# State space heads of a two-layer decoder: the squares of a group summed on VectorE ahead of one product with ones, and the decay block off the diagonal made by ScalarE alone

## The chip, the cores and the metric

The kernel runs on one core of a Trainium2 chip. The metric is the device time of one execution in microseconds (us). A core has TensorE (PE in the profile; PEld are its weight loads), VectorE (DVE), ScalarE (ACT), GpSimd (POOL) and SyncE (SP), each with a queue of its own, which run their instructions in order and wait for one another by semaphores.

## The reference, cut to what matters

A decoder of two layers on 8 sequences of 256 tokens with 256 channels: a state space mixer, cross attention and a gated layer, then self attention, cross attention and a layer of 64 experts, each with a layer norm behind it. Only the first, the state space mixer, is touched by the change. It has 32 heads of 128 channels in 8 groups of norms:

```python
proj = x @ in_proj_w.T
gate, hbc, dt = jnp.split(proj, [I, I + CD], axis=-1)
hbc = silu(conv(hbc, width 4) + conv_b)
hs, B, C = jnp.split(hbc, [I, I + G * N], axis=-1)
dt = softplus(dt + dt_bias); A_bt = -exp(A_log) * dt
# per head, with cum the running sum of A_bt over a sequence:
#   y[l] = sum over s <= l of (C[l] . B[s]) * exp(cum[l] - cum[s]) * dt[s] * X[s]  +  D * X[l]
...
gs = I // G                       # 512 channels, 4 heads
h32 = y * silu(gate)
g = h32.reshape(b, s, I // gs, gs)
var = jnp.mean(g * g, axis=-1, keepdims=True)
h32 = (g * rsqrt(var + EPS)).reshape(b, s, I)
return norm_w * h32 @ out_proj_w.T
```

The line on y is a summary: the reference works it out in chunks of 32 tokens, and the kernel over all 256.

## The kernel before

`mamba_stage` runs `mamba_dt` (dt and its running sums, as rows `cum_rows` in memory and as columns `dtc`), then two passes, each of `mamba_bc` (the masked products C.B into `cb`) and `mamba_heads` (4 groups of 4 heads). The stage takes the first 1280 us; what follows is not touched.

`mamba_heads` goes in steps: a step is one group and one pair of sequences (n counts steps, 16 in a pass), and in it four turns, one for each head j. `head_turns` writes the loop, `slot` gives each engine in each turn its parts, each for a head so many turns ahead: TensorE `project` (3 ahead), `scan` (1), `turn` (2), `out` (0); ScalarE `decays` (2), `square` (0), `activate` (3), `weigh` (2), `tanh` (3); VectorE `finish` (0), `silu` (2), `conv` and `open_` (3); GpSimd `match` (2), `argue` (3). This order, written by hand, is the order of each queue.

For one head: `project` makes px (the head's channels) and pz (its gate), each two products of 512 columns. ScalarE makes pre from px and tz from pz, VectorE runs three taps of the convolution on pre (`conv_taps`), and makes gate from tz and xs from tx, ScalarE's tanh of pre. `turn` transposes xs into pxt, and `weigh` scales it by dt/2 to xt. GpSimd's `argue` writes the arguments cum[l] - cum[s], with the smaller of that and 0 taken, into `decay`, ScalarE takes the exponential in place, and GpSimd's `match` multiplies with `cb` into mix. The block of a sequence is 256 source tokens by 256 targets, of which 384 columns are kept: columns 0 to 255 (`0:S`) are source tokens 0 to 127 with all targets, columns 256 to 383 (`S:TRI`) source tokens 128 to 255 with the second 128 targets. So columns 128 to 255 (`P:S`) are the block off the diagonal. `scan` multiplies xt with mix to py, `finish` makes y and h = y x gate, `square` makes sq = h^2, and `out` adds to po (h times the output weights) and to pss, the sum of squares over channels, by a product of sq with a column of ones.

At the start of a step VectorE reads pss of the last step (`variance`), GpSimd makes the root (`root`), and VectorE scales po with it and adds to x_rows (`add`). GpSimd's `group` at a group's start makes h_d and h_wo from the new weights, and y of head 0 waits for it. SyncE loads the running sums (`cum`) into two buffers cumb, and the weights of each group.

Of the kernel before, what the change touches and what calls it, by code (L numbers as in the profile page):

```python
# [108 lines left out]
def mamba_stage(nc, a, r):  # L109

    with ExitStack() as ctx:
        def sb(name, shape, dt=F32):
            return ctx.enter_context(nc.sbuf_tensor(name, shape, dt))

        def sem(name):
            return ctx.enter_context(nc.semaphore(name))  # L120

        cum_rows = nc.dram_tensor("cum_rows", (H, T), F32, kind="Internal").ap()
        cb = sb("cb", [P, NP * GH, 2, TRI])
        dtc = sb("dtc", [P, NT, 2 * H])
        mamba_dt(nc, a, r, cum_rows, dtc)
        for half in range(2):
            mamba_bc(nc, a, r, half, cb)
            mamba_heads(nc, a, r, half, cum_rows, dtc, cb)


def mamba_dt(nc, a, r, cum_rows, dtc):

    with ExitStack() as ctx, ExitStack() as ctx2:
# [62 lines left out]
        def _(dve):  # L196
# [242 lines left out]
def mamba_heads(nc, a, r, half, cum_rows, dtc, cb):  # L439
# [9 lines left out]
    with ExitStack() as ctx, ExitStack() as ctx2:  # L449
# [20 lines left out]
        cumb = [sb(f"cumb{i}", [P, HG, 2, S]) for i in range(2)]  # L470
        sel = [sb(f"sel{i}", [P, TW, 2, HG]) for i in range(2)]
        decay = [sb(f"decay{i}", [P, 2, TRI]) for i in range(HG)]
# [58 lines left out]
        def _(sp):  # L531
# [9 lines left out]
            def cum(s):  # L541

                sp.wait_ge(argued, LEAD + (s.n - 1) * HG)
                sp.dma_start(cumb[s.vb][:].rearrange("p j u l -> p j (u l)"),
                             cum_rows[bass.ds((s.g * 2 + half) * HG, HG), bass.ds(s.p * 2 * S, 2 * S)].partition_broadcast(P)).then_inc(cums[s.vb], 16)
# [10 lines left out]
        def _(pool):  # L556
# [12 lines left out]
            def argue(s, j, h):  # L569

                pool.wait_ge(cums[s.vb], (s.g * (NP // 2) + s.two + 1) * 16)
                pool.wait_ge(picked, LEAD + s.n + 1)
                for u in range(2):
                    pool.tensor_scalar(decay[j][:, u, 0:S], cumb[s.vb][:, j, u, :], sel[s.vb][:, u * TPB, 1, j:j + 1], 0.0,  # L574
                                       ALU.subtract, ALU.min)
                    ins = pool.tensor_scalar(decay[j][:, u, S:TRI], cumb[s.vb][:, j, u, P:S], sel[s.vb][:, u * TPB + 1, 1, j:j + 1], 0.0,  # L576
                                             ALU.subtract, ALU.min)
                ins.then_inc(argued, 1)
# [27 lines left out]
        def _(pe):  # L606
# [36 lines left out]
            def out(s, j, h):  # L643
                pe.wait_ge(finished, LEAD + h + 1)
                pe.wait_ge(squared, LEAD + h + 1)
                if j == 0:
# [3 lines left out]
                for t in range(TW):  # L650

                    pe.matmul(po[t // TPB][:, t % TPB, :], hh[j % 2][:, t * P:(t + 1) * P], w_out[s.pg][:, j, :],  # L652
                              start=(j == 0 and t % TPB == 0), stop=(j == HG - 1), skip_group_check=True)
                    mm = pe.matmul(pss[:, t:t + 1], sq[j % 2][:, t * P:(t + 1) * P], r.ones[:, 0:1],  # L654
                                   start=(j == 0 and t == 0), stop=(j == HG - 1), skip_group_check=True)
                mm.then_inc(outed, 1)
# [12 lines left out]
        def _(act):  # L669
# [49 lines left out]
        def _(dve):  # L719
            for one in po:  # L720
                dve.memset(one[:], 0.0)
            dve.memset(pss[:, 0:TW], 0.0)
            for one in (picked, convolved, opened, silued, finished):
                dve.drain().then_inc(one, LEAD)
# [26 lines left out]
            def finish(s, j, h):  # L751
# [23 lines left out]
            def body(prev, cur, nxt):  # L775
                for j in range(HG):
# [2399 lines left out]
```

## Time and profile before

| what | value |
|---|---|
| time, median of 3 runs | 3485.99 us (3485.69 to 3489.45) |
| profiled execution, its own time | 3490.39 us |
| its span, first to last instruction | 3488.6 us |
| granted TensorE clock over the span | 0.833 |
| TensorE busy | 2766.1 us, 79% |
| VectorE, ScalarE, GpSimd busy | 1854.6 us (53%), 1553.7 us (45%), 1204.1 us (35%) |
| the squares' products, 1024 instructions, first and last start | 180.0 and 1280.8 us |

The busy shares are means over stages that differ; the two passes over the heads lie from 151 to 665 us and from 769 to 1284 us. A product of 32-bit numbers is two instructions to TensorE, each with a weight load, so the profile counts 1024 where the code has 512.

### The profile page before, as it was taken

Reading aid. Unit: us, or ns where it says so; the run is one execution under the profiler, and the core shown is the slowest. Engines: PE = TensorE matmul, PEld = TensorE weight load, DVE = VectorE, ACT = ScalarE, POOL = GpSimd, SP = SyncE. Lnnn points to the kernel's source line nnn. Section 1 sums busy time; section 2 is a strip of 40 time slices with the busy share of each in tenths; the row PEclk is TensorE's granted clock in tenths of the full one; section 3 lists DMA queues with packets and bytes.
Section 4 is the critical chain, followed back from the end, with each engine's and each line's share of the span. In section 5 each row is a group of like instructions: output and inputs, shape, how many; then the busy total and the mean of one; then the engine's idle time right before and its main releaser. Section 6 shows DMA issues by size and latency. Waiting matters only on the chain. (4 is left out here: it accounts for less than half of the span.)

```text
span 3488.6 us, 49109 instructions
## 1 busy us (share of the span) xinstructions
PE 2766.1 (79%) x13661; PEld 1696.1 (49%) x13663; DVE 1854.6 (53%) x4142; ACT 1553.7 (45%) x3112; POOL 1204.1 (35%) x1132
## 2 busy tenths in 40 slices
PE   5799999879999975887887937887477525988884
PEld 2477777646777753444444513333344212455552
DVE  4676666666666656767773156774322510222334
ACT  3555555455555543767771115665155200123331
POOL 1477777437777740000000021000100063144443
PEclk8999999989999985555557957998679755899997
DMA  1122111012122106500000000000000051377875
GB/s 61 46 55 51 34 51 37 7 49 55 27 53 55 37 12 208 170 1 0 1 1 29 0 17 1 1 1 1 21 1 0 1 179 69 69 163 169 180 172 124
DMA packets 127079, 192.70 MB, mean 55 GB/s; under 512 B 17552, under 2 KB 88208, under 8 KB 125584
## 3 DMA queue, kind: packets, MB, share of 16 engines
q1 hardware_dynamic: 83696, 134.71, 13.7%
q0 software_dynamic: 23616, 33.24, 5.4%
q10 hardware_dynamic: 19584, 22.57, 2.4%
q8 instruction: 83, 1.36, 0.2%
q14 instruction: 100, 0.82, 0.1%
HBM read 123.23 MB, written 67.25 MB: 55 GB/s over the span
## 5 line engine op out<-in xcount | busy, mean ns | idle before, releaser
L228 DVE SCALAR_TENSOR_TENSOR h_pre<-h_px,h_par,h_pre 128x510 f32<-128x510 f32 (+2 forms) x384 | 286.5, 746 | 270.6 <-ACT h_pre L689 250.7
L843 POOL TENSOR_TENSOR norm_rstd<-norm_mv,mhalf 128x4 f32<-128x4 f32 x24 | 28.2, 1177 | 1023.3 <-DVE norm_mv L826 1023.3
L652 PE MATMUL h_po<-h_wo,h_h 128*128 128x256 f32 x1024 | 329.3, 412 | 0.0
L2906 POOL DMA_INDIRECT moe_sums<-ex_y,ex_sidx x132 | 204.8, 1552 | 321.1 <-DVE ex_y L3074 302.9
L574 POOL TENSOR_SCALAR h_decay<-h_cumb,h_sel 128x256 f32<-128x256 f32 x256 | 292.0, 1141 | 25.4 <-DMA h_cumb<-cum_rows 25.4
L585 POOL TENSOR_TENSOR h_mix<-h_decay,cb 128x768 f32<-128x768 f32 x128 | 232.9, 1820 | 166.3 <-ACT h_decay L675 166.3
L616 PE MATMUL h_px<-x_cols,h_w 128*128 128x512 f32 x512 | 254.4, 620 | 25.6 <-DMA h_d<-d_skip 25.6
L1256 ACT ACTIVATE xq_ex<-xq_ps,xq_nmax,xq_qs 128x512 f32<-128x512 f32 x256 | 199.4, 779 | 113.6 <-DVE xq_nmax L1324 113.0
L621 PE MATMUL h_pz<-x_cols,h_w 128*128 128x512 f32 x512 | 242.4, 596 | 5.7 <-DVE h_gate L742 5.6
L1322 DVE TENSOR_REDUCE xq_top<-xq_ps 128x1 f32<-128x512 f32 x256 | 176.3, 689 | 83.5 <-PE xq_ps L1169 81.7
L701 ACT ACTIVATE h_xt<-h_pxt,h_sel 128x128 f32<-128x128 f32 x512 | 146.4, 369 | 152.2 <-PE h_pxt L640 152.2
L2951 PE MATMUL ex_pg<-ex_w,ex_xT 128*128 x528 | 193.5, 489 | 23.0 <-DVE ex_h L3070 8.2
L654 PEld LDWEIGHTS h_pss<-ones,h_sq 128*128 128x128 f32 x1024 | 195.1, 191 | 26.5
L1176 PE MATMUL xq_pa<-identb,xq_pr 128*128 128x128 bf16 x1024 | 149.8, 299 | 61.2 <-DVE xq_pr L1329 60.4
L576 POOL TENSOR_SCALAR h_decay<-h_cumb,h_sel 128x128 f32<-128x128 f32 x256 | 182.5, 713 | 0.0
L689 ACT ACTIVATE h_pre<-h_px,h_par 128x512 f32<-128x512 f32 x128 | 99.6, 778 | 172.6 <-PE h_px L616 165.3
L3064 DVE COPY ex_wt<-ex_xg 128x1 f32 x132 | 20.3, 154 | 274.1 <-DMA moe_sums<-ex_y,ex_sidx 271.1
L621 PEld LDWEIGHTS h_pz<-x_cols,h_w 128*128 128x128 f32 x512 | 97.6, 192 | 132.0 <-issue 121.3
L631 PE MATMUL h_py<-h_mix,h_xt 128*128 128x256 f32 x512 | 155.0, 385 | 7.2 <-DVE h_h L760 7.1
L2053 DVE TENSOR_REDUCE at_nmax<-at_pd 128x4 f32<-128x1024 f32 (+1 forms) x96 | 117.4, 1223 | 79.2 <-PE at_pd L1783 77.0
L652 PEld LDWEIGHTS h_po<-h_wo,h_h 128*128 128x128 f32 x1024 | 155.9, 192 | 0.1
L2967 PE MATMUL ex_po<-ex_wd,ex_hT 88*128 x528 | 142.7, 393 | 16.3 <-issue 13.7
(390 smaller groups left out, 6004.6 us busy)
## 6 DMA issues: line engine op xcount, KB each, us to landing
h_cumb<-cum_rows SPq DMA_DIRECT2D x32, 1024.0 KB, 8.6
moe_tiles<-blank SPq DMA_DIRECT2D x4, 6642.0 KB, 44.1
ex_w<-moe_w SPq DMA_DIRECT2D x64, 352.0 KB
ex_xg<-moe_tiles ACTq DMA_DIRECT2D x136, 162.0 KB
ex_wd<-moe_wd SPq DMA_DIRECT2D x64, 176.0 KB
h_w<-w_xg SPq DMA_DIRECT2D x8, 1024.0 KB, 10.4
moe_sums<-blank SPq DMA_DIRECT2D x2, 2176.0 KB, 26.7
h_wo<-w_out SPq DMA_DIRECT2D x8, 512.0 KB, 10.3
```

The source lines that it names most:

```text
L228: ins = dve.scalar_tensor_tensor(out=out[:, :, back:S], in0=src[:, :, 0:S - back], scalar=par[:, at + CK - 1 - back:at + CK - back], in1=o ...
L574: pool.tensor_scalar(decay[j][:, u, 0:S], cumb[s.vb][:, j, u, :], sel[s.vb][:, u * TPB, 1, j:j + 1], 0.0, ALU.subtract, ALU.min)
L576: ins = pool.tensor_scalar(decay[j][:, u, S:TRI], cumb[s.vb][:, j, u, P:S], sel[s.vb][:, u * TPB + 1, 1, j:j + 1], 0.0, ALU.subtract, ALU.min)
L585: pool.tensor_tensor(mix[j % 2][:], decay[j][:], cbj, ALU.mult).then_inc(matched, 1)
L616: mm = pe.matmul(px[j % 2][:].rearrange("p u l -> p (u l)"), w_in[s.pg][:, k, j, 0, :], r.xT[:, k, bass.ds(s.p * 2 * S, 2 * S)], start=(k ...
L621: mm = pe.matmul(pz[:], w_in[s.pg][:, k, j, 1, :], r.xT[:, k, bass.ds(s.p * 2 * S, 2 * S)], start=(k == 0), stop=(k == KE - 1))
L652: pe.matmul(po[t // TPB][:, t % TPB, :], hh[j % 2][:, t * P:(t + 1) * P], w_out[s.pg][:, j, :], start=(j == 0 and t % TPB == 0), stop=(j = ...
L654: mm = pe.matmul(pss[:, t:t + 1], sq[j % 2][:, t * P:(t + 1) * P], r.ones[:, 0:1], start=(j == 0 and t == 0), stop=(j == HG - 1), skip_gro ...
L1256: act.activation(ex[m % 4][:], ps[m % 2][:], ACT.Exp, bias=nmax[s.par][:, m:m + 1], scale=qs[s.par][:, m:m + 1], accum_out=tot[s.par][:, m ...
L1322: dve.tensor_reduce(top[:, m:m + 1], ps[m % 2][:], AX.X, ALU.max, negate=True)
L2906: pool.indirect_dma_start(out=r.sums[i % 2][:, :], out_offset=bass.IndirectOffsetOnAxis(ap=sidx[i][:, 0:1], axis=0), in_=y[i % 2][:], in_o ...
L2951: mm = pe.matmul(pgu[n][:, 0:2 * FE], xT[n][:, k, :], w[:, bass.ds(lane, 1), k, :].rearrange("p a f -> p (a f)"), start=(k == 0), stop=(k ...
```

## The change

Two edits in `mamba_heads`, and one that prepares for them in `mamba_dt`. First, `out` no longer multiplies each head's squares with ones. The square of a group's first head goes to a new tile `sqsum`, VectorE adds those of the other three heads to it (a new part `gather`, behind `silu` and ahead of `conv` in each turn but the first), and `out` of the last head multiplies the sum with ones, behind its four po. Second, `argue` leaves out the block off the diagonal, and `decays` makes it from `cumb` with the negated cum[s] as a bias, which `dtc` and `sel` hold as a third column; the exponential of the rest is one instruction over the two diagonal blocks. The load of `cumb` waits for the decays, since ScalarE reads `cumb` as well.

```diff
@@ mamba_dt
+                dve.tensor_scalar(dtc[:, 8 * i:8 * i + 8, 2 * H:3 * H], pt[i][:, :, H:2 * H], -1.0, None, ALU.mult)
@@ cum
-                sp.wait_ge(argued, LEAD + (s.n - 1) * HG)
+                sp.wait_ge(decayed, LEAD + (s.n - 1) * HG)
@@ argue
-                    pool.tensor_scalar(decay[j][:, u, 0:S], cumb[s.vb][:, j, u, :], sel[s.vb][:, u * TPB, 1, j:j + 1], 0.0,
-                                       ALU.subtract, ALU.min)
-                    ins = pool.tensor_scalar(decay[j][:, u, S:TRI], cumb[s.vb][:, j, u, P:S], sel[s.vb][:, u * TPB + 1, 1, j:j + 1], 0.0,
-                                             ALU.subtract, ALU.min)
+                    for n in range(TPB):
+                        ins = pool.tensor_scalar(decay[j][:, u, n * S:n * S + P], cumb[s.vb][:, j, u, n * P:(n + 1) * P],
+                                                 sel[s.vb][:, u * TPB + n, 1, j:j + 1], 0.0, ALU.subtract, ALU.min)
@@ out
-                pe.wait_ge(squared, LEAD + h + 1)
...
-                    mm = pe.matmul(pss[:, t:t + 1], sq[j % 2][:, t * P:(t + 1) * P], r.ones[:, 0:1],
-                                   start=(j == 0 and t == 0), stop=(j == HG - 1), skip_group_check=True)
+                if j == HG - 1:
+
+                    pe.wait_ge(summed, LEAD + (s.n + 1) * (HG - 1))
+                    for t in range(TW):
+                        mm = pe.matmul(pss[:, t:t + 1], sqsum[s.vb][:, t * P:(t + 1) * P], r.ones[:, 0:1],
+                                       start=(t == 0), stop=(t == TW - 1), skip_group_check=True)
@@ decays
-                act.activation(decay[j][:], decay[j][:], ACT.Exp).then_inc(decayed, 1)
+                own = decay[j][:].rearrange("p u (n l) -> p u n l", l=P)[:, :, 0:3:2, :]
+                act.activation(own, own, ACT.Exp)
+                for u in range(2):
+                    ins = act.activation(decay[j][:, u, P:S], cumb[s.vb][:, j, u, P:S], ACT.Exp, bias=sel[s.vb][:, u * TPB, 2, j:j + 1])
+                ins.then_inc(decayed, 1)
@@ square
-                act.wait_ge(outed, LEAD + h - 1)
-                act.activation(sq[j % 2][:], hh[j % 2][:], ACT.Square).then_inc(squared, 1)
+                if j == 0:
+                    act.wait_ge(outed, LEAD + (s.n - 1) * HG)
+                else:
+                    act.wait_ge(summed, LEAD + s.n * (HG - 1) + j - 2)
+                act.activation(sqsum[s.vb][:] if j == 0 else sq[j % 2][:], hh[j % 2][:], ACT.Square).then_inc(squared, 1)
@@ VectorE
+            def gather(s, j, h):
+                if j:
+                    dve.wait_ge(squared, LEAD + h + 1)
+                    dve.drain()
+                    dve.tensor_tensor(sqsum[s.vb][:], sqsum[s.vb][:], sq[j % 2][:], ALU.add).then_inc(summed, 1)
...
-                    slot(((3, conv), (3, open_)), cur, nxt, j)
+                    slot(((0, gather), (3, conv), (3, open_)), cur, nxt, j)
```

On TensorE, a turn of the first step before, from its transposes to the next turn's first product (L640 the transposes, L652 po, L654 pss, L616 px):

```order
L640 MATMUL h_pxt<-ident,h_xs 128x128 x4
L652 MATMUL h_po<-h_wo,h_h 128x256
L654 MATMUL h_pss<-ones,h_sq 128x1
L652 MATMUL h_po<-h_wo,h_h 128x256
L654 MATMUL h_pss<-ones,h_sq 128x1
...
L616 MATMUL h_px<-x_cols,h_w 128x512 x2
```

The same place now, in the third and the fourth turn of a step (L642 the transposes, L653 po, L659 pss, L618 and L623 px and pz, L633 and L634 py):

```order
L642 MATMUL h_pxt<-ident,h_xs 128x128 x4
L653 MATMUL h_po<-h_wo,h_h 128x256 x4
L618 MATMUL h_px<-x_cols,h_w 128x512 x2
L623 MATMUL h_pz<-x_cols,h_w 128x512 x2
L633 MATMUL h_py<-h_mix,h_xt 128x256
L634 MATMUL h_py<-h_mix,h_xt 128x128
...
L642 MATMUL h_pxt<-ident,h_xs 128x128 x4
L653 MATMUL h_po<-h_wo,h_h 128x256 x4
L659 MATMUL h_pss<-ones,h_sqsum 128x1 x4
```

Three turns of a step have only po behind the transposes, and the fourth has all four pss in a row behind its po.

On VectorE, the second turn of the first step before, from y on (L755 y, L760 h, L748 xs, L228 the taps, L742 gate):

```order
L755 SCALAR_TENSOR_TENSOR h_y<-h_xs,h_d,h_py 128x512
L760 TENSOR_TENSOR h_h<-h_y,h_gate 128x512
L748 SCALAR_TENSOR_TENSOR h_xs<-h_tx,h_pre 128x512
L228 SCALAR_TENSOR_TENSOR h_pre<-h_px,h_par,h_pre 128x2x255
L228 SCALAR_TENSOR_TENSOR h_pre<-h_px,h_par,h_pre 128x2x254
L228 SCALAR_TENSOR_TENSOR h_pre<-h_px,h_par,h_pre 128x2x253
L742 SCALAR_TENSOR_TENSOR h_gate<-h_tz,h_pz 128x512
```

The same turn now (L767 y, L772 h, L760 xs, L778 the new sum, L229 the taps, L754 gate):

```order
L767 SCALAR_TENSOR_TENSOR h_y<-h_xs,h_d,h_py 128x512
L772 TENSOR_TENSOR h_h<-h_y,h_gate 128x512
L760 SCALAR_TENSOR_TENSOR h_xs<-h_tx,h_pre 128x512
L778 TENSOR_TENSOR h_sqsum<-h_sqsum,h_sq 128x512
L229 SCALAR_TENSOR_TENSOR h_pre<-h_px,h_par,h_pre 128x2x255
L229 SCALAR_TENSOR_TENSOR h_pre<-h_px,h_par,h_pre 128x2x254
L229 SCALAR_TENSOR_TENSOR h_pre<-h_px,h_par,h_pre 128x2x253
L754 SCALAR_TENSOR_TENSOR h_gate<-h_tz,h_pz 128x512
```

The sum stands between xs and the taps, so the taps are queued behind its wait for the square.

## Rows read from the trace of the kernel before

**Rows 1.** Busy time by stretch: us, PE, PEld, DVE, ACT, POOL, clock, DMA.

```profile
1024.00:1149.00 125.00, 125.00 (x578) 89.47 (x577) 85.39 (x149) 69.44 (x145) 94.70 (x87) 1.00 0.19 47
...
299.35:330.55 31.20, 31.20 (x147) 22.32 (x146) 22.64 (x39) 17.45 (x38) 23.12 (x21) 1.00 0.20 34
```

**Rows 2.** Timeline: start us, us, engine, line; TensorE over one turn.

```profile
307.15 1.96 PE L616 MATMUL h_px<-x_cols,h_w 128*128 128x512 f32 x4
...
308.95 1.88 PE L621 MATMUL h_pz<-x_cols,h_w 128*128 128x512 f32 x4
...
310.67 0.59 PE L631 MATMUL h_py<-h_mix,h_xt 128*128 128x256 f32 x2
...
311.98 0.60 PE L640 MATMUL h_pxt<-ident,h_xs 128*128 128x128 f32 x4
...
312.41 0.60 PE L652 MATMUL h_po<-h_wo,h_h 128*128 128x256 f32 x2
...
312.85 0.28 PE L654 MATMUL h_pss<-ones,h_sq 128*128 128x1 f32 x2
...
312.99 0.68 PE L652 MATMUL h_po<-h_wo,h_h 128*128 128x256 f32 x2
...
314.95 1.96 PE L616 MATMUL h_px<-x_cols,h_w 128*128 128x512 f32 x4
```

**Rows 3.** The page's costliest groups: weight loads, additions of squares' products.

```profile
L654 PEld LDWEIGHTS h_pss<-ones,h_sq 128*128 128x128 f32 x1024 | 195.1, 191 | 26.5
```

**Rows 4.** Waits of TensorE in the first pass over heads.

```profile
PE h_py L631 <- DVE h_h L760: 3.6, 1, 3.6
PE h_pz L621 <- DVE h_gate L742: 2.8, 2, 1.8
```

**Rows 5.** Timeline, VectorE over one turn.

```profile
312.27 0.68 DVE L742 SCALAR_TENSOR_TENSOR h_gate<-h_tz,h_pz 128x512 f32<-128x512 f32 x1
...
312.87 0.74 DVE L755 SCALAR_TENSOR_TENSOR h_y<-h_xs,h_d,h_py 128x512 f32<-128x512 f32 x1
...
313.68 0.78 DVE L760 TENSOR_TENSOR h_h<-h_y,h_gate 128x512 f32<-128x512 f32 x1
...
314.39 0.68 DVE L748 SCALAR_TENSOR_TENSOR h_xs<-h_tx,h_pre 128x512 f32<-128x512 f32 x1
...
317.77 2.39 DVE L228 SCALAR_TENSOR_TENSOR h_pre<-h_px,h_par,h_pre 128x510 f32<-128x510 f32 x3 [2.70 <-ACT h_pre L689]
```

**Rows 6.** Timeline, ScalarE over one turn.

```profile
312.67 1.15 ACT L701 ACTIVATE h_xt<-h_pxt,h_sel 128x128 f32<-128x128 f32 x4 [1.21 <-PE h_pxt L640]
...
313.69 0.64 ACT L706 ACTIVATE h_tx<-h_pre 128x512 f32<-128x512 f32 x1
...
314.30 0.84 ACT L675 ACTIVATE h_decay<-h_decay 128x768 f32<-128x768 f32 x1
...
315.05 0.61 ACT L681 ACTIVATE h_sq<-h_h 128x512 f32<-128x512 f32 x1
...
316.95 0.78 ACT L689 ACTIVATE h_pre<-h_px,h_par 128x512 f32<-128x512 f32 x1 [1.29 <-PE h_px L616]
```

**Rows 7.** GpSimd's three groups of the heads, from the page.

```profile
L574 POOL TENSOR_SCALAR h_decay<-h_cumb,h_sel 128x256 f32<-128x256 f32 x256 | 292.0, 1141 | 25.4 <-DMA h_cumb<-cum_rows 25.4
L585 POOL TENSOR_TENSOR h_mix<-h_decay,cb 128x768 f32<-128x768 f32 x128 | 232.9, 1820 | 166.3 <-ACT h_decay L675 166.3
...
L576 POOL TENSOR_SCALAR h_decay<-h_cumb,h_sel 128x128 f32<-128x128 f32 x256 | 182.5, 713 | 0.0
```

**Rows 8.** Timeline: the first head's y; a group block of GpSimd; the update behind it.

```profile
174.70 0.75 DVE L755 SCALAR_TENSOR_TENSOR h_y<-h_xs,h_d,h_py 128x512 f32<-128x512 f32 x1 [3.94 <-POOL h_wo L566]
...
297.35 1.90 POOL L566 TENSOR_TENSOR h_wo<-h_wo,h_par 128x1024 f32<-128x1024 f32 x1
...
302.39 1.66 DVE L771 SCALAR_TENSOR_TENSOR x_rows<-h_po,h_rstd,x_rows 128x256 f32<-128x256 f32 x4 [0.62 <-POOL h_rstd L590]
```

**Rows 9.** One line's instructions: min, median, max ns, 180 to 1270 us.

```profile
L760 DVE TENSOR_TENSOR h_h<-h_y,h_gate x125: 691/693/873, 183.1 to 1269.2; 128x512 f32<-128x512 f32 x125
```

More of the change, by code:

```diff
@@ L123, in mamba_stage @@
         cb = sb("cb", [P, NP * GH, 2, TRI])
-        dtc = sb("dtc", [P, NT, 2 * H])
+        dtc = sb("dtc", [P, NT, 3 * H])
         mamba_dt(nc, a, r, cum_rows, dtc)
@@ L470, in mamba_heads @@
         cumb = [sb(f"cumb{i}", [P, HG, 2, S]) for i in range(2)]
-        sel = [sb(f"sel{i}", [P, TW, 2, HG]) for i in range(2)]
+        sel = [sb(f"sel{i}", [P, TW, 3, HG]) for i in range(2)]
         decay = [sb(f"decay{i}", [P, 2, TRI]) for i in range(HG)]
@@ L483, in mamba_heads @@
         sq = [sb(f"sq{i}", [P, 2 * S]) for i in range(2)]
+        sqsum = [sb(f"sqsum{i}", [P, 2 * S]) for i in range(2)]
         var = sb("var", [P, TW])
@@ L511, in mamba_heads @@
         squared = sem("squared")
+        summed = sem("summed")
         outed = sem("outed")
@@ L650, in out @@
                 for t in range(TW):
-                    pe.matmul(po[t // TPB][:, t % TPB, :], hh[j % 2][:, t * P:(t + 1) * P], w_out[s.pg][:, j, :],
-                              start=(j == 0 and t % TPB == 0), stop=(j == HG - 1), skip_group_check=True)
-                    mm = pe.matmul(pss[:, t:t + 1], sq[j % 2][:, t * P:(t + 1) * P], r.ones[:, 0:1],
-                                   start=(j == 0 and t == 0), stop=(j == HG - 1), skip_group_check=True)
+                    mm = pe.matmul(po[t // TPB][:, t % TPB, :], hh[j % 2][:, t * P:(t + 1) * P], w_out[s.pg][:, j, :],
+                                   start=(j == 0 and t % TPB == 0), stop=(j == HG - 1), skip_group_check=True)
+                if j == HG - 1:
[3 more added lines that the diff above has]
+                                       start=(t == 0), stop=(t == TW - 1), skip_group_check=True)
                 mm.then_inc(outed, 1)
@@ L722, in _ @@
             dve.memset(pss[:, 0:TW], 0.0)
-            for one in (picked, convolved, opened, silued, finished):
+            for one in (picked, convolved, opened, silued, finished, summed):
                 dve.drain().then_inc(one, LEAD)
@@ L730, in select @@
                     ins = dve.tensor_copy(sel[s.vb][:, t, :, :],
-                                          dtc[:, bass.ds(s.p * TW + t, 1), :].rearrange("p a (c h) -> p (a c) h", c=2)[:, :, bass.ds((s.g * 2 + half) * HG, HG)])
+                                          dtc[:, bass.ds(s.p * TW + t, 1), :].rearrange("p a (c h) -> p (a c) h", c=3)[:, :, bass.ds((s.g * 2 + half) * HG, HG)])
                 ins.then_inc(picked, 1)
```

## The prediction, made before the changed kernel had run

> **What bounds the kernel now.** I read the busy time by stretch first. In a stretch from the middle of the second pass over the heads TensorE is busy for the whole 125.00 us at a granted clock of 1.00, while VectorE has 85.39 us of work, ScalarE 69.44 and GpSimd 94.70 [rows 1]. One step (two batch items, one group of four heads) is 31.20 us long and TensorE is busy for 31.20 of them [rows 1]: the reader is to see that no other engine sets the pace. The waits say the same: over 505 us of the first pass TensorE waited 3.6 us once and 2.8 us twice [rows 4].
>
> So the time of the heads is the sum of what TensorE issues, and I price that from its timeline over one turn (one head of a step). From one px to the next is 7.80 us [rows 2]: px 1.80 (307.15 to 308.95), pz 1.72 (to 310.67), py 1.31 (to 311.98), the four transposes 0.43 (to 312.41), and `out`, four pairs of po and pss, 2.54 (to 314.95). There are 128 turns in 32 steps.
>
> **What leaves TensorE.** pz streams two products of 512 columns in 1.72, so a product of 256 columns is 0.43, and the four of po should be 1.72. That leaves 2.54 - 1.72 = 0.82 for the four pss. px, the product behind the last pss, takes 1.80 where its twin pz takes 1.72; I put these 0.08 to pss too. A turn without pss is then 1.72 + 1.72 + 1.31 + 0.43 + 1.72 = 6.90 us, 0.90 less. Three turns of each step lose it: 96 x 0.90 = 86.4 us.
>
> The fourth turn keeps four pss, now back to back, which no row shows. Each is two instructions with a weight load each, 1024 loads for 512 products [rows 3]. The nearest rows are the transposes, which also load weights for each: 0.43 for four, 0.11 each [rows 2]. Eight take 0.88, and with the 0.08 for px the turn is 6.90 + 0.96 = 7.86, which is 0.06 more than now. From below, a pair takes 0.14 from its start to the next po [rows 2]; four take 0.56, the turn 0.32 less, and 10 us are gained on top. From above, a load lasts 0.191 us [rows 3]; with nothing overlapped eight take 1.53, the turn 0.65 more again, and 32 x 0.65 = 21 us of the gain are gone. I take 0.11, since a pss between po products now costs a pair 0.20 of TensorE's time, which is two of these. Step: 3 x 6.90 + 7.86 = 28.56 against 31.20. Term: 32 x 2.64 = 84.5 us.
>
> Here a page has another figure. The Trainium skill ("TensorE: Matmul & The Clock Gate", Back-to-back issue gap) gives about 81 ns for each pair of weight load and 128-column matmul in a sustained stream; the row here has 0.11. By the page the eight would take 0.65 and the whole gain would be an estimated 7 us larger; the measurement decides.
>
> **What comes to VectorE.** Each of the turns 1 to 3 gets one sum of 128x512, both operands in SBUF, with a drain ahead. Its like is h = y x gate, 693 ns in the median [rows 9], 0.71 from start to start [rows 5]. VectorE's turn today, start to start: gate 0.60, y 0.81, h 0.71, xs about 0.65, three taps 2.3; that is 5.1 of 7.80, and with the sum 5.8 to 5.9 of 6.90. Cover: VectorE now stands idle for 2.70 us ahead of the taps, waiting for ScalarE's pre [rows 5]. Behind the sum in the queue stand the taps and gate of the head three ahead, and TensorE's next pz waits for gate.
>
> Does the sum end before pre does? Count from the start of a px. The transposes begin at 4.75 in the shorter turn, and ScalarE's four xt follow 0.69 later as now (311.98 to 312.67): at 5.44. xt takes 1.02 to the next start, tx about 0.55 [rows 6], so the decays start at 7.0. Today decay, 768 columns, takes 0.75 to the next start. Its new form is one call of 512 columns (like the square, 0.61 long, about 0.52 to the next start) and two of 128 (like xt, 1.02 / 4 = 0.255): 1.03, 0.28 more. Bound from above: pre has bias and scale by partition and takes 0.78, 0.17 more than the square; with 0.17 on both calls, 0.34 more. The square then starts at 8.03 and ends at 8.64, which is 1.74 of the next turn. h was done at about 7.3, so it is not late. The sum runs from about 1.85 to 2.6. pre starts at 2.00, when px has landed, and the taps at 2.82 as now (317.77 against 314.95). The sum fits with 0.2 to spare. If it is 0.3 late, the taps end at 5.5 and gate at 6.2, and pz of the next turn wants gate at 8.62: 2.4 us of cover. py of the next turn wants h at 10.35 and has it at 7.6. I cost the sum and the calls at nothing. Without this cover each would cost its length: 96 x 0.75 = 72 us and 128 x 0.28 = 36 us.
>
> The square of turn 0 goes to the sum's own tile. TensorE no longer waits for the squares, except in turn 3: the sum is there at 2.6 of the turn, pss wants it at 6.9.
>
> **GpSimd.** A head's arguments are now four of 128 columns instead of two of 256 and two of 128: 2 x (1141 - 713) = 856 ns less; the other 713s stay and the mix, 1820, too [rows 7]. A turn goes from 5.53 to 4.67 us. Steady, this is worth nothing, since the mix is ready almost a turn before py. It counts in the ramp of each pass: the first head's y waits for GpSimd's last piece in the opening, h_wo, with VectorE idle for 3.94 us [rows 8], and TensorE's one long wait, 3.6 us, is for the h that follows [rows 4]. On that chain lie two argument blocks behind the first decay (-1.71) and two decays on ScalarE, 0.28 to 0.35 longer (+0.65): 1.0 us sooner, twice: 2 us. The new negated copy in dtc is two small VectorE instructions once, under 0.68 each (the 512-column gate [rows 5]): up to 1 us, and I take 0.7.
>
> **What gets tight.** In a group's first step the update of x_rows, whose wait is for GpSimd's root, ends at 302.39 + 1.66 = 304.05 [rows 8]; the step starts at 299.35 [rows 1], so this is at 4.70, and `out` of turn 0, which waits for it, is at 5.26 now and at 5.18 after. The group's first y waits for h_wo; GpSimd's group block comes behind turn 3's arguments, and by the sum above (decays until 1.13, mix 1.82, arguments 2.85, group block with h_wo's 1.90 [rows 8] about 2.05, a hand-over of 0.1) ends at 7.95 of a turn of 7.86, where now it ends 0.1 ahead of the turn's end (299.25 against 299.35): 0.2 later. The update is then at 4.9: 0.3 spare, in 8 steps of 32. The loads of cumb now wait for the decays instead of the arguments, 2 to 4 us later in a double-buffered ring with a step of 28 us: nothing.
>
> **Sum.** 84.5 + 2.0 - 0.7 = 85.8 us. The profiled execution took 3490.39 us for a span of 3488.60, and the median of the timed runs is 3485.99, 4.4 lower; the saving is the same against each: span 3403, profiled time 3405, median **3400 us**.
>
> **Rivals.**
> (a) The forecast: TensorE stays the bound. 3390 to 3412 by the bounds of the fourth turn (0.56 for its pss at the low end, half of the unoverlapped loads at the high one). Chance 0.80.
> (b) VectorE and GpSimd get in each other's way. For: the sum is a second instruction per turn with two SBUF operands, and GpSimd works 68% of a turn. If a sum were held back for a whole mix, 1.82, it would end at 4.4, the taps at 6.8, gate at 7.4, h at 9.0, and the round over square, sum and taps would be about 7.1 for 6.90: 96 x 0.2 = 19 us lost, 3419; with every VectorE instruction of this sort held as well, up to 3440. Against: h itself is such an instruction and in 125 cases beside a busy GpSimd was at 693 in the median and 873 at most [rows 9], so the hold is at most 0.18. The Trainium skill ("SBUF — State Buffer", SBUF: two separate sides) calls the port pair an exclusive lock between a VectorE instruction with two SBUF inputs and a GpSimd instruction that reads SBUF; these rows show no such block. Chance 0.10.
> (c) The back-to-back pss overlap nothing: 3400 + 21 = 3421. Chance 0.06.
> (d) Slower than before: ScalarE. The round taps, tx, decays, square, sum, taps is 2.39 + 0.64 + 1.03 + 0.61 + 0.75 and four hand-overs of about 0.1, 5.8 us. It decides from the point where it passes 6.90 and ends slower beyond 7.80, that is if the three decay calls take 3.0 instead of 1.03. At 1.1 us each the turn is 8.1 and the time 3486 + 128 x 0.3 = 3524. For: nothing here has a bias on a decay. Against: pre has one, at 0.78 for 512 columns [rows 6]. Chance 0.03.
> (e) No change: something else holds the turn at 7.80 even now. Against: TensorE busy for 31.20 of 31.20. Chance 0.01.
>
> **Range.** (a) with half of (b) and (c): 3390 to 3422. A change of 0.2% (7 us) is about what a measurement tells here. Faster 0.96, same 0.01, slower 0.03.
>
> **What would show it.** Turns 6.90 apart in three of four and about 7.86 in the fourth; pss 256 instructions instead of 1024, starts 0.11 apart; TensorE still busy for whole stretches at clock 1.00; the sum at about 0.7 us, ending before the taps are released by pre. Wrong would be: waits of TensorE for gate or h in each turn, VectorE waiting for the square beyond pre's end, taps that follow the sum and not pre, GpSimd's rows longer, or a fourth turn above 8.3.

## The result, and the profile after

The changed kernel takes 3441.77 us (median of 4 runs, 3434.61 to 3448.74) against 3487.72 for the kernel before beside it (3485.69 to 3490.55): ratio 0.9868, 95% interval 0.9846 to 0.989. It is faster by 46 us, little more than half of the 86 that were forecast, and lies above the range.

| | before | after |
|---|---|---|
| profiled execution, its own time | 3490.39 us | 3442.29 us |
| span | 3488.6 us | 3440.4 us |
| TensorE clock over the span | 0.833 | 0.827 |
| TensorE, VectorE, ScalarE, GpSimd busy | 2766.1, 1854.6, 1553.7, 1204.1 us | 2692.6, 2039.9, 1601.5, 1169.4 us |
| first px to last px, first and second pass | 491.9, 493.3 us | 465.7, 468.1 us |

The last line is read from the timeline of TensorE's products px, 64 a pass, and serves for all comparisons below: it holds the two passes and nothing of the stages behind them. A step should have fallen from 31.20 to 28.56 us. In the first pass 15 steps from px to px are 28.52 to 31.88, most of them 29.0 to 29.5.

VectorE's busy time grew by 185 us, where 96 sums of 0.69 are 66. Busy time by stretch, in the middle of the two passes (us, TensorE, its loads, VectorE, ScalarE, GpSimd, clock, DMA), against [rows 1]:

```profile
182.50:616.00 433.50, 426.64 (x1771) 290.18 (x1769) 400.63 (x582) 276.50 (x647) 331.06 (x314) 1.00 0.20 46
771.00:1210.00 439.00, 429.29 (x1772) 290.70 (x1773) 404.15 (x587) 277.23 (x650) 333.31 (x318) 1.00 0.19 45
```

TensorE is no longer busy all the time: 426.64 of 433.50 and 429.29 of 439.00. VectorE is at 92%. Three of the page's costliest groups, against [rows 7] (GpSimd's arguments, its mix, and the new sum):

```profile
L578 POOL TENSOR_SCALAR h_decay<-h_cumb,h_sel 128x128 f32<-128x128 f32 x512 | 398.9, 793 | 26.2 <-DMA h_cumb<-cum_rows 26.2
...
L587 POOL TENSOR_TENSOR h_mix<-h_decay,cb 128x768 f32<-128x768 f32 x128 | 264.3, 2064 | 159.8 <-ACT h_decay L683 159.8
...
L778 DVE TENSOR_TENSOR h_sqsum<-h_sqsum,h_sq 128x512 f32<-128x512 f32 x96 | 151.2, 1575 | 17.3 <-ACT h_sq L693 14.2
```

The sum's mean is 1575 ns, not 693. GpSimd's pieces of 128 columns grew from 713 to 793, its mix from 1820 to 2064. Each piece is as large as before or as its like, so the time added is not work of its own. The same by line, minimum, median and maximum in ns, for xs and for the sum:

```profile
L760 DVE SCALAR_TENSOR_TENSOR h_xs<-h_tx,h_pre x128: 680/684/2357, 158.6 to 1220.7; 128x512 f32<-128x512 f32 x128
```

```profile
L778 DVE TENSOR_TENSOR h_sqsum<-h_sqsum,h_sq x96: 691/2059/2071, 183.9 to 1230.0; 128x512 f32<-128x512 f32 x96
```

Most are either at their own length or at one length far above it: 62 of the 96 sums and 30 of the 128 xs are more than 0.15 us above their shortest, and none of the 128 h. The timeline of a turn shows what the upper length is (all engines, some rows left out):

```profile
299.44 1.88 PE L618 MATMUL h_px<-x_cols,h_w 128*128 128x512 f32 x4
...
301.15 0.69 DVE L772 TENSOR_TENSOR h_h<-h_y,h_gate 128x512 f32<-128x512 f32 x1
...
301.76 0.68 DVE L760 SCALAR_TENSOR_TENSOR h_xs<-h_tx,h_pre 128x512 f32<-128x512 f32 x1
301.78 2.35 POOL L587 TENSOR_TENSOR h_mix<-h_decay,cb 128x768 f32<-128x768 f32 x1 [1.40 <-ACT h_decay L683]
301.88 0.63 ACT L693 ACTIVATE h_sq<-h_h 128x512 f32<-128x512 f32 x1 [0.25 <-DVE h_h L772]
...
302.42 0.76 ACT L701 ACTIVATE h_pre<-h_px,h_par 128x512 f32<-128x512 f32 x1
...
302.61 2.06 DVE L778 TENSOR_TENSOR h_sqsum<-h_sqsum,h_sq 128x512 f32<-128x512 f32 x1 [0.16 <-ACT h_sq L693]
...
304.10 3.22 POOL L578 TENSOR_SCALAR h_decay<-h_cumb,h_sel 128x128 f32<-128x128 f32 x4
...
304.60 2.38 DVE L229 SCALAR_TENSOR_TENSOR h_pre<-h_px,h_par,h_pre 128x510 f32<-128x510 f32 x3
...
306.34 1.88 PE L618 MATMUL h_px<-x_cols,h_w 128*128 128x512 f32 x4
```

xs starts at 301.76, the mix 0.02 later. The mix lasts 2.35 instead of 1.81: it has lost 0.54. The sum is released at 302.61, in the middle of the mix, and ends at 304.67, which is 0.54 behind the end of the mix at 304.13. I read this as a sum that stood still for the rest of the mix and then ran its 512 columns; the runs below test it. The taps start only then, at 304.60, and not 2.82 behind px as in [rows 2, 5] but 5.16. In the fourth turn of this step the mix comes first by 0.02 and xs is held in its place:

```profile
313.25 1.88 PE L618 MATMUL h_px<-x_cols,h_w 128*128 128x512 f32 x4
...
316.03 1.82 POOL L587 TENSOR_TENSOR h_mix<-h_decay,cb 128x768 f32<-128x768 f32 x1 [1.57 <-ACT h_decay L683]
316.05 2.35 DVE L760 SCALAR_TENSOR_TENSOR h_xs<-h_tx,h_pre 128x512 f32<-128x512 f32 x1
...
317.77 0.38 PE L634 MATMUL h_py<-h_mix,h_xt 128*128 128x128 f32 x2
...
318.45 0.42 PEld L642 LDWEIGHTS h_pxt<-ident,h_xs 128*128 128x128 f32 x4 [0.49 <-DVE h_xs L760]
...
318.49 0.69 DVE L778 TENSOR_TENSOR h_sqsum<-h_sqsum,h_sq 128x512 f32<-128x512 f32 x1
...
320.68 0.95 PE L659 MATMUL h_pss<-ones,h_sqsum 128*128 128x1 f32 x8
...
321.49 1.96 PE L618 MATMUL h_px<-x_cols,h_w 128*128 128x512 f32 x4
```

Here the mix keeps its 1.82, xs lasts 2.35, the transposes wait for xs until 318.45 instead of following py, and the turn is 8.24. What TensorE waited for over both passes (total us, times, longest), against 3.6 and 2.8 in the first pass in [rows 4]; "issue" is a wait for which the profile shows no releaser:

```profile
PE h_py L633 <- DVE h_h L772: 11.6, 7, 2.7
PE h_po L653 <- issue: 11.1, 15, 1.2
...
PE h_pxt L642 <- DVE h_xs L760: 5.3, 18, 0.4
PE h_pz L623 <- DVE h_gate L754: 5.1, 4, 2.2
```

### The profile page after: what moved, and what is told of

The parts are those of the page before. It is cut to its first block and busy times, and to the rows that moved or that the text cites. A ratio compares the mean times of both kernels' runs of the same rounds, so it can differ in the third digit from the quotient of the medians.

```text
span 3440.4 us, 47900 instructions
## 1 busy us (share of the span) xinstructions
PE 2692.6 (78%) x12894; PEld 1609.5 (47%) x12895; DVE 2039.9 (59%) x4240; ACT 1601.5 (47%) x3368; POOL 1169.4 (34%) x1132
## 5 line engine op out<-in xcount | busy, mean ns | idle before, releaser
L578 POOL TENSOR_SCALAR h_decay<-h_cumb,h_sel 128x128 f32<-128x128 f32 x512 | 398.9, 793 | 26.2 <-DMA h_cumb<-cum_rows 26.2
L587 POOL TENSOR_TENSOR h_mix<-h_decay,cb 128x768 f32<-128x768 f32 x128 | 264.3, 2064 | 159.8 <-ACT h_decay L683 159.8
L229 DVE SCALAR_TENSOR_TENSOR h_pre<-h_px,h_par,h_pre 128x510 f32<-128x510 f32 (+2 forms) x384 | 285.6, 744 | 52.3 <-ACT h_pre L701 32.0
L618 PE MATMUL h_px<-x_cols,h_w 128*128 128x512 f32 x512 | 247.6, 607 | 25.8 <-DMA h_d<-d_skip 25.8
L653 PE MATMUL h_po<-h_wo,h_h 128*128 128x256 f32 x1024 | 247.9, 386 | 11.1 <-issue 11.1
L623 PE MATMUL h_pz<-x_cols,h_w 128*128 128x512 f32 x512 | 244.3, 600 | 5.1 <-DVE h_gate L754 5.1
L653 PEld LDWEIGHTS h_po<-h_wo,h_h 128*128 128x128 f32 x1024 | 187.0, 193 | 37.9 <-issue 16.7
L633 PE MATMUL h_py<-h_mix,h_xt 128*128 128x256 f32 x512 | 154.0, 383 | 11.6 <-DVE h_h L772 11.6
L778 DVE TENSOR_TENSOR h_sqsum<-h_sqsum,h_sq 128x512 f32<-128x512 f32 x96 | 151.2, 1575 | 17.3 <-ACT h_sq L693 14.2
L623 PEld LDWEIGHTS h_pz<-x_cols,h_w 128*128 128x128 f32 x512 | 97.7, 192 | 132.2 <-issue 95.8
L229 DVE SCALAR_TENSOR_TENSOR b_bc_pre<-b_ps,b_bc_par,b_bc_pre 128x510 f32<-128x510 f32 (+2 forms) x192 | 138.4, 744 | 29.8 <-ACT b_bc_pre L372 19.9
L1280 ACT ACTIVATE xq_prT<-xq_pa 128x512 bf16<-128x512 bf16 x256 | 151.3, 592 | 4.4 <-issue 4.1
```

What stands on the lines that cost most here:

```text
L229: ins = dve.scalar_tensor_tensor(out=out[:, :, back:S], in0=src[:, :, 0:S - back], scalar=par[:, at + CK - 1 - back:at + CK - back], in1=o ...
L578: ins = pool.tensor_scalar(decay[j][:, u, n * S:n * S + P], cumb[s.vb][:, j, u, n * P:(n + 1) * P], sel[s.vb][:, u * TPB + n, 1, j:j + 1], ...
L587: pool.tensor_tensor(mix[j % 2][:], decay[j][:], cbj, ALU.mult).then_inc(matched, 1)
L618: mm = pe.matmul(px[j % 2][:].rearrange("p u l -> p (u l)"), w_in[s.pg][:, k, j, 0, :], r.xT[:, k, bass.ds(s.p * 2 * S, 2 * S)], start=(k ...
L623: mm = pe.matmul(pz[:], w_in[s.pg][:, k, j, 1, :], r.xT[:, k, bass.ds(s.p * 2 * S, 2 * S)], start=(k == 0), stop=(k == KE - 1))
L633: pe.matmul(py[:, u, :], xt[j % 2][:, u * TPB, :], mix[j % 2][:, u, 0:S], start=True, stop=False)
```

## The experiments

The theory to test, **hold**: a VectorE instruction with two inputs in SBUF (the sum, h, xs) and a GpSimd instruction that reads SBUF exclude each other, and the later one stands still for as long as the earlier one lasts. Its rivals: the three decay calls on ScalarE and the wait for the square (**ScalarE**), and the sum's mere length and place in VectorE's order (**VectorE's order**). All ratios are to runs of the kernel before on the same chip, with 95% intervals. The second group of four (mix in two, sum on GpSimd, two with the sum behind gate) ran on another chip, on which the kernel before took 3408.10 us; the passes of the two kernels that were run twice agree within 0.9 us from one chip to another. The expectations for that group are times of the first chip. With their ratios taken to its 3487.72 us, mix in two is 3410, sum on GpSimd 3453, sum behind gate 3440, and the same with old decays 3418.

| run | time, us | ratio (interval) | passes, us |
|---|---|---|---|
| changed kernel | 3441.77 | 0.9868 (0.9846 to 0.989) | 465.7, 468.1 |
| first edit alone | 3449.35 | 0.9898 (0.9869 to 0.9927) | 466.6, 468.3 |
| second edit alone | 3486.72 | 1.0013 (0.9994 to 1.0031) | 491.4, 495.3 |
| no addition | 3385.16 | 0.9719 (0.9686 to 0.9753) | 451.2, 451.8 |
| sum with one SBUF input | 3389.24 | 0.9728 (0.9699 to 0.9757) | 451.3, 452.8 |
| mix in two | 3330.87 | 0.9777 (0.9744 to 0.9809) | 453.0, 453.6 |
| sum on GpSimd | 3368.14 | 0.9901 (0.9862 to 0.9939) | 470.6, 471.2 |
| sum behind gate | 3359.40 | 0.9864 (0.9831 to 0.9896) | 465.3, 465.5 |
| sum behind gate, old decays | 3336.30 | 0.9799 (0.9766 to 0.9833) | 456.1, 458.6 |
| first edit, mix in two | 3482.02 | 0.9995 (0.9979 to 1.0011) | 485.4, 483.8 |
| before, mix in two | 3481.89 | 0.9999 (0.9981 to 1.0018) | 494.0, 493.7 |
| changed kernel again | 3445.15 | 0.9897 (0.9864 to 0.993) | 466.6, 468.9 |
| mix in two again | 3407.74 | 0.9802 (0.9768 to 0.9836) | 453.0, 453.0 |

**First edit alone.** Arguments and decays as before the change:

```diff
-                    for n in range(TPB):
-                        ins = pool.tensor_scalar(decay[j][:, u, n * S:n * S + P], ...
+                    pool.tensor_scalar(decay[j][:, u, 0:S], cumb[s.vb][:, j, u, :], ...
+                    ins = pool.tensor_scalar(decay[j][:, u, S:TRI], cumb[s.vb][:, j, u, P:S], ...
@@ decays
+                act.activation(decay[j][:], decay[j][:], ACT.Exp).then_inc(decayed, 1)
```

> The first edit alone: squares summed on VectorE, one pss per step; arguments and decays as in the kernel before. Hold theory (a VectorE instruction with two SBUF inputs and a GpSimd instruction that reads SBUF exclude each other, so the sum waits out the mix): GpSimd works 5.5 us a turn instead of 4.7, so the sum is still held, its median between 1.2 and 2.1 us, and the time is 3440 to 3470. ScalarE theory (the three decay calls make the round over square and sum too long): the decays are 0.28 us shorter and the turns go to 6.90, time 3400 to 3410, sum at 0.69.

Passes of 466.6 and 468.3, the sum at 1932 ns in the mean. With the old, shorter decays the loss is the same, so ScalarE's new calls are not the cause. Hold foresaw 3440 to 3470. The taps here follow one another by 7.14, 7.14, 7.15 and 7.57 us in most steps behind a group's first, which makes the 29.0 us of such a step: the round from taps to taps, with the held sum in it, sets the pace and not TensorE.

**Second edit alone.** The kernel before with the new `argue` and `decays`, its squares' products kept.

> The second edit alone: GpSimd leaves out the block off the diagonal, ScalarE makes it with a bias; a pss with each po, as in the kernel before. Hold theory: no sum to hold; TensorE keeps its turn of 7.80, time 3483 to 3490; xs may now and then meet the mix, with cover. ScalarE theory: the longer decays show as waits of TensorE for h or gate, time 3490 to 3525.

The turns stay at 7.80, the ratio is 1.0013 with 1 in the interval. The second edit by itself is worth nothing and costs nothing.

**No addition.**

```diff
-                    dve.tensor_tensor(sqsum[s.vb][:], sqsum[s.vb][:], sq[j % 2][:], ALU.add).then_inc(summed, 1)
+                    dve.drain().then_inc(summed, 1)
```

> The changed kernel without the addition itself: the wait for the square, the drain and the semaphore stay, so pss is of the first head's squares alone. Hold theory: VectorE loses 1.57 us in three turns of four, TensorE is the bound again, turns of 6.90, 6.90, 7.7 and 6.9 to 7.0, time 3395 to 3412. ScalarE theory: the wait for the square is what costs and it is kept, so the time stays at 3430 to 3442.

Turns of 6.91, 6.91, 7.71 and 6.99, steps of 28.52, 3385.16 us. The wait for the square is still there, so the wait is not the cause. The time went below what hold foresaw (3395 to 3412).

**Sum with one SBUF input.**

```diff
-                    dve.tensor_tensor(sqsum[s.vb][:], sqsum[s.vb][:], sq[j % 2][:], ALU.add).then_inc(summed, 1)
+                    dve.tensor_tensor(sqsum[s.vb][:, TW:], pss[:, TW:], sq[j % 2][:, TW:], ALU.add).then_inc(summed, 1)
```

> The changed kernel with the sum's first operand read from an idle part of a PSUM bank (508 columns, zeros) instead of SBUF, so the squares are copied and not summed. Same length of work, same waits, one SBUF input. Hold theory: the sum is never held, 0.70 to 0.78 us in the median and at most 0.85, the mix is 1.81 when only the sum meets it, time 3398 to 3415. Rival (the sum's place in VectorE's order and its wait cost the time, whatever it reads): sum still near 2 us from its start to its end or taps as late as now, time 3435 to 3445.

This run decides. The sum's line, and a turn in which it lies wholly inside a mix (timeline):

```profile
L778 DVE TENSOR_TENSOR h_sqsum<-h_pss,h_sq x96: 685/686/689, 184.8 to 1194.1; 128x508 f32<-128x508 f32 x96
```

```profile
304.83 1.81 POOL L587 TENSOR_TENSOR h_mix<-h_decay,cb 128x768 f32<-128x768 f32 x1 [1.40 <-ACT h_decay L683]
...
305.11 0.76 ACT L701 ACTIVATE h_pre<-h_px,h_par 128x512 f32<-128x512 f32 x1
305.30 0.69 DVE L778 TENSOR_TENSOR h_sqsum<-h_pss,h_sq 128x508 f32<-128x508 f32 x1 [0.54 <-ACT h_sq L693]
...
305.90 2.38 DVE L229 SCALAR_TENSOR_TENSOR h_pre<-h_px,h_par,h_pre 128x510 f32<-128x510 f32 x3
```

The mix starts at 304.83 and lasts 1.81; the sum starts in it at 305.30 and lasts 0.69; the taps follow at 305.90. The same engine, place, wait and nearly the same length as in the changed kernel, with one operand read from PSUM: 96 sums at 685 to 689 ns, none held. Steps are 28.52 again and TensorE is busy throughout (busy time by stretch, first pass):

```profile
182.00:602.00 420.00, 420.00 (x1766) 288.84 (x1765) 344.13 (x588) 275.14 (x650) 298.45 (x316) 1.00 0.23 47
```

VectorE's order as a cause falls, and so does ScalarE. Both runs leave out a part of the computation, and both came out below the expected range. The part below the range lies behind the passes: from the last px of the second pass to the end they take 2209.4 and 2208.1 us, against 2236.1 and 2228.5 in the first and the second edit alone on the same chip, and what comes behind the passes works on other values there. Their passes together are 82.2 and 81.2 us shorter than before, where the prediction has 84.5 for the turns and 2 for the ramps.

**Mix in two.**

```diff
-                pool.tensor_tensor(mix[j % 2][:], decay[j][:], cbj, ALU.mult).then_inc(matched, 1)
+                for u in range(2):
+                    ins = pool.tensor_tensor(mix[j % 2][:, u, :], decay[j][:, u, :], cbj[:, u, :], ALU.mult)
+                ins.then_inc(matched, 1)
```

> The changed kernel with GpSimd's mix as two instructions of 384 columns, one for each sequence. Hold theory: what is held waits for one GpSimd instruction and not for the whole mix, so a sum that meets it is 1.1 to 1.6 us instead of 2.06, the round over taps, tanh, decays, mix and sum falls from 7.14 below 6.90, and the time is 3390 to 3415, in spite of about 0.2 us more work for GpSimd in each turn. Rival (the two engines share bandwidth and slow each other in proportion): two pieces are as slow as one, 3440 to 3450.

```profile
303.08 0.61 ACT L695 ACTIVATE h_sq<-h_h 128x512 f32<-128x512 f32 x1
303.32 2.41 POOL L588 TENSOR_TENSOR h_mix<-h_decay,cb 128x384 f32<-128x384 f32 x2 [1.40 <-ACT h_decay L685]
...
303.60 0.76 ACT L703 ACTIVATE h_pre<-h_px,h_par 128x512 f32<-128x512 f32 x1
...
303.80 1.08 DVE L780 TENSOR_TENSOR h_sqsum<-h_sqsum,h_sq 128x512 f32<-128x512 f32 x1 [0.59 <-ACT h_sq L695]
...
304.80 2.37 DVE L229 SCALAR_TENSOR_TENSOR h_pre<-h_px,h_par,h_pre 128x510 f32<-128x510 f32 x3
```

The sum starts 0.48 into the first half and ends at 304.88: held for the rest of one half, about 1 us long, and not for the whole mix. The same holds wherever something is held by a mix or by a half of it: over all runs 304 VectorE instructions that a whole mix held end 0.54 to 0.56 behind it, and 276 that a half held end 0.54 to 0.55 behind that half. Its median is 1076 ns, 61 us of idle time are back between square and sum, and the steps are 28.52 but for a group's first, 29.15. Passes of 453: all but 2 us of what the kernel without a sum has. The ratio is 0.9777 here, and 0.9802 in the second run, where the changed kernel beside it has 0.9897; 3407.74 against 3445.15. It beats both kernels. Slowing each other in proportion, the rival of this run, would have left the sum as it was.

**Sum on GpSimd**, behind the arguments, where GpSimd waits for the decays.

```diff
-                    slot(((0, gather), (3, conv), (3, open_)), cur, nxt, j)
+                    slot(((3, conv), (3, open_)), cur, nxt, j)
-            parts = ((2, match), (3, argue))
+            parts = ((2, match), (3, argue), (0, gather))
```

> The sum moved to GpSimd, behind the arguments, where it waits for the decays anyway; VectorE has its old list. Hold theory: both now exclude h and xs only, GpSimd works 4.7 + 1.3 = 6.0 us of 6.9 and VectorE 5.1; h may be held by the sum for up to 1.3 us and still reach py; 3390 to 3420. Rival (GpSimd becomes the bound, since the sum delays the mix): turns above 7.2, 3440 or more.

A miss: 470.6, no better than on VectorE. Three turns of four are 6.9 to 7.0, but the fourth is 8.65 to 9.47, since GpSimd comes to the sum only behind its arguments and TensorE waits for it (total us, times, longest):

```profile
PE h_pss L665 <- POOL h_sqsum L598: 27.0, 30, 1.5
```

Now it is h that is held, 1132 ns in the mean.

**Sum behind gate.**

```diff
-                    slot(((0, gather), (3, conv), (3, open_)), cur, nxt, j)
+                    slot(((3, conv), (3, open_), (0, gather)), cur, nxt, j)
```

> The changed kernel with the sum behind the taps and gate in VectorE's order instead of ahead of them. There GpSimd is at its arguments, pieces of 0.71 us, and not at the mix. Hold theory: sum 0.69 in most cases and at most 1.4, the turns 6.90, 6.90, 7.7, 7.0, the time 3388 to 3405, about as without the addition. Rival (VectorE's length of work is what costs): no better than now, 3435 to 3445.

The sum was at 728 ns as foreseen, the time was not: ratio 0.9864, expected some 0.974. Most steps are 28.52, but in the step behind most groups' first one turn is 10.16 long. The timeline there:

```profile
311.95 0.69 DVE L778 TENSOR_TENSOR h_sqsum<-h_sqsum,h_sq 128x512 f32<-128x512 f32 x1
...
313.17 1.81 POOL L587 TENSOR_TENSOR h_mix<-h_decay,cb 128x768 f32<-128x768 f32 x1 [1.55 <-ACT h_decay L683]
...
313.38 2.16 DVE L772 TENSOR_TENSOR h_h<-h_y,h_gate 128x512 f32<-128x512 f32 x1
...
315.57 0.63 ACT L693 ACTIVATE h_sq<-h_h 128x512 f32<-128x512 f32 x1 [2.54 <-DVE h_h L772]
...
316.11 0.76 ACT L701 ACTIVATE h_pre<-h_px,h_par 128x512 f32<-128x512 f32 x1
...
316.90 2.39 DVE L229 SCALAR_TENSOR_TENSOR h_pre<-h_px,h_par,h_pre 128x510 f32<-128x510 f32 x3 [0.76 <-ACT h_pre L701]
```

The sum in its new place pushes y and h back, h falls just behind the start of a mix and is held to 2.16. Behind h stand the square, ScalarE's pre (316.11, though px had long landed) and VectorE's taps, and with those the next sum, for which TensorE then waits. What hold foresaw for the sum came true; where it would strike next I had not worked out.

**Sum behind gate, old decays.**

> As the run with the sum behind gate, with arguments and decays as in the kernel before, so the first edit alone with another place for the sum. Hold theory: GpSimd works 5.5 us of 6.9, pieces of 1.14 among them, and the mix comes earlier and meets h; h is held in some turns but mostly in time for py: 3395 to 3430. If the second edit brings nothing, it equals the run with the sum behind gate within 5 us.

Passes of 456.1 and 458.6, 23 us less time than with the new decays. The time is in the range, the way to it is not: I had expected the mix to meet h in some turns, and h is never held (692 ns in the mean). So with the whole mix the second edit is worth what the phase it gives is worth: nothing ahead of gate, a loss behind it. That the phase and nothing else makes this difference is argued from the timelines and not shown by a run of its own.

**First edit, mix in two.**

> The first edit alone (arguments and decays as in the kernel before) with GpSimd's mix in two instructions. It tells whether the second edit earns anything once the hold is short. Hold theory: the sum is held for one piece at most, steps of 28.52 in most places; GpSimd works 5.7 us of 6.9, so a group's first step is later than with the second edit, 31 instead of 29.15: a pass over the heads of 455 to 462 us against 453. If the second edit matters more, 465 or above.

A miss: 485.4 and 483.8, the gain all but gone. GpSimd's three groups (mix halves, arguments of 256 and of 128 columns):

```profile
L589 POOL TENSOR_TENSOR h_mix<-h_decay,cb 128x384 f32<-128x384 f32 x256 | 292.4, 1163 | 100.7 <-ACT h_decay L683 99.3 <-PE h_py L637 1.0 <-issue 0.5
L577 POOL TENSOR_SCALAR h_decay<-h_cumb,h_sel 128x256 f32<-128x256 f32 x256 | 291.9, 1140 | 26.0 <-DMA h_cumb<-cum_rows 26.0
...
L579 POOL TENSOR_SCALAR h_decay<-h_cumb,h_sel 128x128 f32<-128x128 f32 x256 | 246.6, 963 | 0.0
```

In a turn these are 2 x 1.163 + 2 x 1.140 + 2 x 0.963 = 6.5 us, and GpSimd also waits for the decays for 0.8 us: 7.3, beyond 6.90. Of the 6.5, 0.8 is time in which GpSimd's own pieces are lengthened beside VectorE's: undisturbed they are 0.997, 1.141 and 0.713, 5.7 in a turn. Most steps are 30.1. That GpSimd's round is now the bound follows from this sum; no run tests it by itself. Here the second edit counts: with it the passes are 453, without it 485. It takes 0.86 us a turn off GpSimd.

**Control: before, mix in two.**

> Control: the kernel before with GpSimd's mix in two instructions and nothing else. TensorE is its bound, so hold theory and every other say: turns of 7.80, a pass over the heads of 490 to 494 us, the same time as before within 0.2%.

Turns of 7.80, ratio 0.9999. Splitting the mix earns nothing where nothing is held.

**The changed kernel again, and mix in two again.**

> The changed kernel once more, beside the others on one chip: sum 2.06 in the median, a pass over the heads of 465 to 468 us, ratio 0.986 to 0.988.

> The changed kernel with the mix in two instructions, once more beside it on one chip: a pass of 453 us, ratio 0.975 to 0.980, 25 to 35 us below the changed kernel.

The passes are as expected, 466.6 and 453.0, and the sum's median is 1878 instead of 2060 ns, with xs held 43 times instead of 30. The ratios, 0.9897 and 0.9802, lie just above those expected, and the difference of 37 us a little above the 25 to 35 expected.

## Why the prediction was wrong, point by point

- **What bounds the kernel, and TensorE's terms.** Right. Where nothing holds the sum the turns are 6.91, 6.91, 7.72 and 6.99 against 6.90, 6.90, 7.86 and 6.90: a step of 28.52 for 28.56. The eight instructions of pss back to back take 0.81 (320.68 to 321.49) for 0.88. The 0.08 that px loses behind pss fall in the turn that follows, which is 6.99. The 2 us for the ramps are not borne out: with the second edit alone the passes are 491.4 and 495.3, against 491.9 and 493.3 before. Rival (c), pss that overlap nothing, is refuted.
- **The sum on VectorE costs nothing, since it fits ahead of pre.** This is the step that failed. The prediction put the sum at 0.7 us, from 1.85 to 2.6 of a turn, and ended the argument there. (Its place was near enough: where nothing holds it, in the turn of px at 309.79 of the run with one SBUF input, it starts at 1.91. One reading on the way was 0.06 short: tx takes 0.61 to the next start in [rows 6], not 0.55.) It is 1.58 in the mean, because at 1.2 to 3.0 of the turn, by the prediction's own count for GpSimd, lies the mix.
- **"The hold is at most 0.18".** This is the reading that let the step fail. [rows 9] shows 125 h at 693 and at most 873, and I took them for instructions beside a busy GpSimd. GpSimd is busy for 71% of a turn, but at h it is idle or at its arguments, never at the mix. GpSimd's timeline in the turn of [rows 2, 5]:

```profile
307.07 0.70 POOL L576 TENSOR_SCALAR h_decay<-h_cumb,h_sel 128x128 f32<-128x128 f32 x1
308.79 1.86 POOL L585 TENSOR_TENSOR h_mix<-h_decay,cb 128x768 f32<-128x768 f32 x1 [1.03 <-ACT h_decay L675]
...
313.54 0.73 POOL L576 TENSOR_SCALAR h_decay<-h_cumb,h_sel 128x128 f32<-128x128 f32 x1
315.29 1.81 POOL L585 TENSOR_TENSOR h_mix<-h_decay,cb 128x768 f32<-128x768 f32 x1 [1.02 <-ACT h_decay L675]
```

h starts at 313.68, 0.14 into the last piece of the arguments, and takes 0.78 beside it; xs at 314.39 ends before the mix at 315.29. Most h and xs lie at the end of the arguments or in the gap behind them, in which GpSimd waits for the decays, since the decays stand behind the tanh on ScalarE for which xs waits as well. Matching the starts over both passes, none of the 125 h and none of the 125 xs begins inside a mix. The 873 itself is an h that begins 0.04 into a piece of the arguments:

```profile
188.97 0.71 POOL L576 TENSOR_SCALAR h_decay<-h_cumb,h_sel 128x128 f32<-128x128 f32 x1
189.01 0.87 DVE L760 TENSOR_TENSOR h_h<-h_y,h_gate 128x512 f32<-128x512 f32 x1
```

So 0.18 was a true price for meeting an argument piece, and the prediction carried it over to the mix, which no h had met and which costs up to 1.66.
- **Rival (b)** is what happened, with 0.10. Its mechanism, a sum held for a whole mix, was right, its price was half: 19 us for rounds of 7.1. Its upper bound, 3440 with h and xs held as well, is near the measured 3441.77, but h was never held and xs in 30 turns of 128, so this nearness is in part luck. The round is taps, tanh, decays, mix, sum, taps, and it is 7.14 in the plain turns (taps at 304.60 and 311.74); missed were xs, which makes the mix 0.54 longer or is itself held and keeps the transposes waiting (turns of 8.24), and the group starts (up to 9.37 where 7.0 was due). The Trainium skill ("SBUF — State Buffer", Who interferes with whom) states that such a VectorE instruction and a GpSimd instruction that reads SBUF exclude each other, whichever starts first keeps the port for the whole instruction, and one with a single SBUF input does not contend. For the mix the trace agrees: 2.06 with two inputs, 0.686 with one, and both orders of who waits. For the pieces of the arguments it does not, and there the measurement decides: the h above ends 0.20 behind its piece, not 0.54, and other VectorE instructions run through such a piece at their own length (see the last section). The prediction set the rule aside on the strength of [rows 9].
- **ScalarE, rival (d).** The three decay calls are near what was costed, 614 ns and twice 386 in the median. The Trainium skill ("ScalarE: Activation LUTs", What ACT_TABLE_LOAD costs) gives 280 ns + 0.833 ns a column with a bias from a pointer, which makes an estimate of 387 for 128 columns; the trace agrees. They cost nothing in the second edit alone.
- **GpSimd's 0.86 us less is worth nothing, steady.** Right for the kernel before and for the change as it is; with the mix in two, a kernel that the prediction did not speak of, it is the difference between 453 and 485.

## What to carry to other kernels

A row that shows an instruction undisturbed proves only that it was undisturbed where it stood. Before one puts a VectorE instruction with two SBUF inputs into a stretch, one looks at what GpSimd runs in just that stretch. If it is a product of two tiles like the mix, the whole length of that instruction is the price; the pieces of the arguments, which read one tile and one value per partition, cost at most 0.3 us here. Where the meeting can't be avoided, the cheap remedies are an operand from PSUM, or a GpSimd instruction cut in pieces: what is held waits for one piece.

## What the runs showed that I had not expected

- What GpSimd does matters, not only that it reads SBUF. In the kernel before, 7 h and 2 xs begin 0.04 to 0.14 us into an argument piece and lose 0.08 to 0.29; the 33 that begin 0.37 us or more into one lose nothing. In the changed kernel 30 sums begin 0.65 us or more into an argument piece and take their 0.69, and it is that piece which is 1.15 long instead of 0.71, though it had started first. Over all runs, none of the 758 h, xs and sums with two inputs in SBUF that begin inside an argument piece is longer than 0.98. Why the arguments hold so much less than the mix stays open.
- A hold is as sharp as a few hundredths of a microsecond: with xs first by 0.02 the mix loses 0.54, with the mix first by 0.02 xs loses 1.66. By the records the border is not at zero: in the changed kernel 26 xs that begin 15 to 20 ns behind a mix still go first, and 30 that begin 19 to 23 ns behind one are held. So turns of one kernel differ by a microsecond and more, in a pattern that repeats with the steps.
- A held instruction's time in the profile contains the hold. Busy VectorE at 92% looks like work; its median and maximum by line show that it is not.
- Cutting one 768-column product of GpSimd in two cost 0.18 us a turn (1.81 to 2 x 0.997 in the control) and earned 13 to 16 us a pass.
